# Four-layer decoder on one core: the first attention layer without zero-padded rows, row maxima in two parts, value bias behind the softmax

## The reference

```python
x = x + tanh(g_xattn[l]) * attention_l(layernorm(x), ctx)
x = x + tanh(g_ffn[l])   * feed_forward_l(layernorm(x))
```

```python
q = Wq @ xn + bq;  k = Wk @ ctx + bk;  v = Wv @ ctx + bv      # (128, 256)
p = softmax(q.T k / sqrt(8)) per head;  out = Wo @ (p v) + bo
```

## Time and profile before

| | us |
|---|---|
| median of 3 runs | 1309.64 (1308.12 to 1316.08) |
| profiled execution | 1303.64 |
| its span (first to last instruction) | 1301.7 |
| mean granted TensorE clock | 0.859 of full |
| busy in the span: PE / PEld | 971.2 / 569.7 |
| busy in the span: DVE / ACT / POOL | 685.3 / 439.5 / 376.7 |

### The profile page before, as it was taken

The page is one execution under the profiler, slowest core; times in us unless marked ns, Lnnn a source line. Parts: engine busy times, 40 slices in busy tenths (PEclk is TensorE's granted clock), DMA queues, the critical chain, the costliest instruction groups (busy, mean ns, idle before and its releaser), DMA issues.

```text
span 1301.7 us, 19061 instructions
## 1 busy us (share of the span) xinstructions
PE 971.2 (75%) x6613; PEld 569.7 (44%) x6613; DVE 685.3 (53%) x1700; ACT 439.5 (34%) x718; POOL 376.7 (29%) x516
## 2 busy tenths in 40 slices
PE   1768896788168799577747771598989999559993
PEld 1334453677124345455425651134444544326662
DVE  4858774443378614267662233787878783301111
ACT  4245554211025520244311330035555657212220
POOL 3112210222555100334204004325555656220002
PEclk9989988799669999788657995569989999679997
DMA  5444633364544100644332764201010000530002
GB/s 133 111 94 103 166 103 115 130 227 150 151 113 122 30 24 0 170 74 86 61 129 97 195 180 143 68 6 38 2 38 1 2 2 2 226 126 25 17 13 73
DMA packets 117257, 115.43 MB, mean 89 GB/s; under 512 B 71758, under 2 KB 107342, under 8 KB 113742
## 3 DMA queue, kind: packets, MB, share of 16 engines
q1 hardware_dynamic: 110924, 102.94, 28.8%
q0 software_dynamic: 3072, 8.39, 2.1%
q10 hardware_dynamic: 3168, 2.88, 0.7%
HBM read 88.22 MB, written 29.62 MB: 91 GB/s over the span
## 4 chain that ended last, share of the span: by engine, by line
PE 44%; DVE 18%; issue 9%; DMA 5%; POOL 3%; ACT 2%; SPq 1%; POOLq 0%; DVEq 0%; ACTq 0%
PE psT L1373 6%; PE psT L1083 5%; PE psB L1083 5%; PE psT L1226 4%; PE psB L1192 4%; DVE mxp L1739 4%; PE psO L1270 3%; PE psB L1387 3%; DVE mxp L1743 3%; DMA xn<-scr_sorted 2%; PE psB L1414 2%; PE psB L1438 2%; PE psO L1260 2%; PE psT L1336 1%; PE psB L1091 1%
## 5 line engine op out<-in xcount | busy, mean ns | idle before, releaser
L1519 ACT ACTIVATE Pt<-psT 128x1024 f32<-128x1024 f32 x192 | 195.9, 1023 | 138.8 <-PE psT L1226 136.9
L1739 DVE TENSOR_REDUCE mxp<-psB 128x1 f32<-128x512 f32 x256 | 162.4, 685 | 41.6 <-PE psB L1192 40.4
L1226 PE MATMUL psT<-whole 99*128 99x256 bf16 (+1 forms) x1024 | 156.5, 279 | 10.3 <-issue 10.0
L1743 DVE TENSOR_REDUCE mxp<-psB 128x2 f32<-128x512 f32 x192 | 122.6, 684 | 40.5 <-PE psB L1198 40.1
L1198 PE MATMUL psB<-whole 96*128 96x256 bf16 x384 | 76.9, 308 | 66.3 <-issue 53.3
L1226 PEld LDWEIGHTS psT<-whole 99*128 99x128 bf16 (+1 forms) x1024 | 97.8, 103 | 60.2 <-issue 28.1
L2057 POOL TENSOR_TENSOR rstd<-vare,cst 128x1 f32<-128x1 f32 x64 | 35.9, 563 | 288.9 <-DVE vare L1658 288.6
L1192 PE MATMUL psB<-whole 96*128 96x512 bf16 x256 | 97.5, 438 | 4.8 <-DVE mxp L1739 3.5
L1091 PE MATMUL psB<-cst,xn 128*128 128x128 f32 x96 | 22.9, 330 | 82.3 <-DVE xn L1598 82.0
L1373 PE MATMUL psT<-whole,qf 128*128 x176 | 80.7, 602 | 0.6 <-ACT qf L1558 0.6
L1198 PEld LDWEIGHTS psB<-whole 96*128 96x128 bf16 x384 | 30.2, 105 | 116.4 <-issue 75.7
(11 more groups left out here) (295 smaller groups left out, 1788.6 us busy)
## 6 DMA issues: line engine op xcount, KB each, us to landing
whole<-in_w SPq DMA_DIRECT2D x6, 3072.0 KB, 10.6
whole<-in_w SPq DMA_DIRECT2D x32, 512.0 KB, 4.8
scr_q<-sq SPq DMA_DIRECT2D x48, 96.0 KB, 1.9
scr_k<-sk SPq DMA_DIRECT2D x48, 96.0 KB, 1.9
whole<-scr_q SPq DMA_DIRECT2D x64, 64.0 KB
whole<-scr_k SPq DMA_DIRECT2D x64, 64.0 KB
xn<-scr_sorted SPq DMA_DIRECT2D x31, 128.0 KB, 3.0
scr_sorted_out<-xn SPq DMA_DIRECT2D x31, 128.0 KB, 2.7
```

The lines of the kernel that those rows point to most:

```text
L1226: ins = pe.matmul(psT[:, s.n % 2, i * A.T:(i + 1) * A.T], lhsT=k_at[:, h * kw + s.c * P:h * kw + (s.c + 1) * P], rhs=q_at[:, h * A.T:(h + ...
L1519: act.activation(p_slot(A, s.p)[:, 0:4 * A.T], psT[:, s.n % 2, 0:4 * A.T], ACT.Exp).then_inc(T_used[s.n % 2], 1)
L1739: dve.tensor_reduce(mxp[:, s.un.g % 2, at:at + 1], psB[:, s.n % BANKS, :], AX.X, ALU.max).then_inc(bank_used[s.n % BANKS], 1)
L1743: dve.tensor_reduce(mxp[:, s.un.g % 2, at:at + 2], psB[:, s.n % BANKS, :].rearrange("p (h n) -> p h n", h=2), AX.X, ALU.max).then_inc(bank ...
```

## The change

Six edits, here in the order of the code:

- `Layer` gets `rows` = 6d and `lows`, the number of parts of the maximum: 3 in layer 3, 2 in layers 0 and 1, none in layer 2. The maxima matmul of layer 0 has 48 rows, the score matmul 50; in layers 1, 2 and 3 they have 96, and 98, 96 and 99.
- The steps `zero` go. GpSimd fills the whole value buffer and its ones columns before its first wait.
- negsplit works from the maxima directly: two VectorE operations for two parts, four for three. negmax has two or three DMAs; ln 255 becomes the bias of layer 3's exponential.
- The value bias leaves the values. Since each row of probabilities sums to one, it is a constant per output channel: Wo @ bv. In `prepare` TensorE transposes the row `bv0`, in the new step `bias_out` it multiplies by Wo, and VectorE adds `bo0` and applies the gate. A new step `bias`, one a unit, adds the column to `x` on GpSimd.
- fv of layer 0 is copied by ScalarE; oy of layer 0 is one VectorE operation on `x`.
- Normalising is one operation over both position tiles.

The diff, with little of what stands around each edit; the new fields of `Layer`, the declarations of the tile `ln255` (128x1) and of semaphores, and the count `neg_after` of the DMAs that a wait on the maxima needs are left out.

```diff
@@ -110,7 +110,8 @@
     return Layer(layer=layer, H=heads, d=d, U=units, nb=batches, TC=tcs, T=tcs * P,
-                           NC=chunks, has_max=has_max, G=heads // 4, halves=heads * d // P, parts=2 if layer == 3 else 1)
+                           NC=chunks, has_max=has_max, G=heads // 4, halves=heads * d // P, parts=2 if layer == 3 else 1,
+                           rows=6 * d, lows=(3 if layer == 3 else 2) if has_max else 0)
@@ -418,10 +419,11 @@
                         (packs, u + at["packs"], u + at["packs"] + 0.02)]
+            if A.layer == 0:
+                streams += [([lambda r=units[u]: add("bias", un=r)], u + at["body"], u + at["body"])]
             if A.layer == 0 and u == 0:
-                streams += [([lambda i=i: add("zero", i=i)], w, w)
-                            for i, w in ((0, 0.5 * at["front"]), (1, at["max"] + 0.2), (2, at["max"] + 0.5))]
-                streams += [([lambda: add("prepare")], at["front"], at["front"]),
+                streams += [([lambda: add("prepare", m=take("M"))], at["front"], at["front"]),
+                            ([lambda: add("bias_out", m=take("M"))], at["max_first"], at["max_first"]),
                             ([lambda i=i: add("loads", i=i) for i in range(LOADS)], 2.0, 9.5)]
@@ -934,7 +943,8 @@
                         for r in range(4 if A.layer == 3 else 3):
-                            sp.dma_start(KP[96:99, 4096 * r:4096 * (r + 1)], t["ones3"]).then_inc(k_ones, 16)
+                            sp.dma_start(KP[A.rows:A.rows + A.lows, 4096 * r:4096 * (r + 1)], t["ones3"][0:A.lows, :]
+                                         ).then_inc(k_ones, 16)
                 elif s.kind == "vstore":
@@ -1020,9 +1030,6 @@
                     sp.wait_ge(q_stored[u.g % 2], 32 * (u.g // 2 + 1))
-                    if A.layer == 0 and u.u < 3:
-                        sp.wait_ge(q_zeroed, u.u + 1)
-                        sp.wait_ge(k_zeroed, 2 * (u.u + 1))
                     pack(sp, A, QP[:, u.g % 3, :], scratch(dq, A, u.g), A.T, q_packed[u.g % 2], is_q=True)
@@ -1034,8 +1041,8 @@
                     turn(sp, bank_used, s.m)
-                    for p3 in range(3):
-                        r = 96 + p3
+                    for p3 in range(A.lows):
+                        r = A.rows + p3
                         HP = A.H // A.parts
@@ -1117,6 +1124,12 @@
                     pe.wait_ge(const_in, 16 * 6)
+                    pe.transpose(m_begin(s.m)[:, 0:P], row("bv0"), ident).then_inc(bank_ready[s.m % BANKS], 1)
+                elif s.kind == "bias_out":
+                    dst = m_begin(s.m)
+                    pe.wait_ge(bias_made, 1)
+                    pe.matmul(dst[:, 0:1], lhsT=w_at0[:, 3, :], rhs=colx[:, 3:4], start=True, stop=True
+                              ).then_inc(bank_ready[s.m % BANKS], 1)
                 elif s.kind == "kp":
@@ -1181,7 +1194,7 @@
                 elif s.kind == "smax":
-                    A, u, K = s.A, s.un, 96
+                    A, u, K = s.A, s.un, s.A.rows
                     if s.first:
@@ -1203,16 +1216,16 @@
                     pe.wait_ge(neg_split, s.i + 1)
-                    w = 3 * A.H // A.parts
+                    w = A.lows * A.H // A.parts
                     for tc in range(A.TC):
                     A, u = s.A, s.un
-                    K = 99 if A.has_max else 96
+                    K = A.rows + A.lows
                     if s.neg is not None:
-                        pe.wait_ge(neg_in[s.neg % 2], 48 * (s.neg // 2 + 1))
+                        pe.wait_ge(neg_in[s.neg % 2], neg_after[s.neg])
                     if s.first:
@@ -1451,12 +1464,6 @@
                     act.activation(tg[:, 0:8], rows[:, 0:8], ACT.Tanh).then_inc(gates_done, 1)
-                elif s.kind == "zero":
-
-                    at = 6144 + 2048 * s.i
-                    for p in (32, 64):
-                        act.activation(arena[p:p + 32, at:at + 2048], const("zero")[p:p + 32, :].to_broadcast([32, 2048]),
-                                       ACT.Copy).then_inc(k_zeroed, 1)
                 elif s.kind == "kt":
@@ -1489,6 +1496,14 @@
                     ins.then_inc(bank_used[s.m % BANKS], 1)
+                elif s.kind == "fv" and s.A.layer == 0:
+                    turn(act, bank_ready, s.m)
+                    if s.un.u == 0:
+                        act.wait_ge(v_set, 1)
+                    if s.done_before >= 0:
+                        act.wait_ge(PV_done, s.done_before + 1)
+                    act.activation(VA[:, s.un.g % 3, 0:32, 0:8], m_slot(s.m).rearrange("p (h d) -> p h d", d=8), ACT.Copy
+                                   ).then_inc(bank_used[s.m % BANKS], 1)
                 elif s.kind == "fqt":
@@ -1500,8 +1515,8 @@
                     if s.i >= 2:
-                        act.wait_ge(neg_in[s.i % 2], 48 * (s.i // 2))
-                    w = 3 * A.H // A.parts
+                        act.wait_ge(neg_in[s.i % 2], neg_after[s.i - 2])
+                    w = A.lows * A.H // A.parts
                     act.activation(nmT[0:w, s.i % 2, 0:A.T], m_slot(s.m).bitcast(BF16)[0:w, 0:A.T],
@@ -1516,7 +1531,9 @@
                         turn(act, T_ready, s.n)
-                        act.activation(p_slot(A, s.p)[:, 0:4 * A.T], psT[:, s.n % 2, 0:4 * A.T], ACT.Exp).then_inc(T_used[s.n % 2], 1)
+                        bias = ln255[:, :] if A.layer == 3 else 0.0
+                        act.activation(p_slot(A, s.p)[:, 0:4 * A.T], psT[:, s.n % 2, 0:4 * A.T], ACT.Exp, bias=bias
+                                       ).then_inc(T_used[s.n % 2], 1)
                 elif s.kind == "oev":
@@ -1656,14 +1673,6 @@
                     dve.tensor_scalar(vare[:, b:b + 1], mv[:, b, 1:2], EPS, None, ALU.add).then_inc(var_ready, 1)
-                elif s.kind == "zero":
-
-                    at = 2048 * s.i
-                    link(dve.memset(arena[32:64, at:at + 2048], 0.0))
-                    dve.memset(arena[64:96, at:at + 2048], 0.0).then_inc(q_zeroed, 1)
-
-                    link(dve.memset(VA[:, s.i, :, :], 0.0))
-                    link(dve.memset(VA[:, s.i, :, SUMCOL:SUMCOL + 1], 1.0))
                 elif s.kind == "vblocks":
@@ -1676,6 +1685,16 @@
                     link(dve.tensor_scalar(tg[:, 10:11], tg[:, 6:7], 0.1, None, ALU.mult))
+                    turn(dve, bank_ready, s.m)
+                    dve.tensor_copy(colx[:, 3:4], m_slot(s.m)[:, 0:1]).then_inc(bank_used[s.m % BANKS], 1)
+                    evacuated(dve, s.m)
+                    dve.sem_inc(bias_made, 1)
+                elif s.kind == "bias_out":
+                    turn(dve, bank_ready, s.m)
+                    dve.tensor_scalar(colx[:, 3:4], m_slot(s.m)[:, 0:1], col("bo0"), tg[:, 0:1], ALU.add, ALU.mult
+                                      ).then_inc(bank_used[s.m % BANKS], 1)
+                    evacuated(dve, s.m)
+                    dve.sem_inc(bias_made, 1)
                 elif s.kind == "kp":
@@ -1716,21 +1735,14 @@
                     normalise(s.xn)
-                elif s.kind == "fv":
+                elif s.kind == "fv" and s.A.layer == 2:
                     A, n = s.A, s.m
                         dve.wait_ge(PV_done, s.done_before + 1)
-                    if A.layer == 0:
-                        for c in range(2):
-                            ins = dve.tensor_tensor(VA[:, s.un.g % 3, c * 16:(c + 1) * 16, 0:8],
-                                                    m_slot(n)[:, c * P:(c + 1) * P].rearrange("p (h d) -> p h d", d=8),
-                                                    row("bv0").rearrange("p (h d) -> p h d", d=8), ALU.add)
-                    else:
-                        ins = dve.tensor_tensor(VA[:, s.un.g % 3, 0:16, 0:16],
-                                                m_slot(n).rearrange("p (h d) -> p h d", d=16),
-                                                row("bv2").rearrange("p (h d) -> p h d", d=16), ALU.add)
-                    ins.then_inc(bank_used[n % BANKS], 1)
+                    dve.tensor_tensor(VA[:, s.un.g % 3, 0:16, 0:16], m_slot(n).rearrange("p (h d) -> p h d", d=16),
+                                      row("bv2").rearrange("p (h d) -> p h d", d=16), ALU.add
+                                      ).then_inc(bank_used[n % BANKS], 1)
                 elif s.kind == "smax":
@@ -1754,16 +1766,20 @@
 
-                    link(dve.tensor_scalar(nm[:, 0, 0:w], mx, -1.0, LN255 if A.layer == 3 else 0.0, ALU.mult, ALU.add))
                     if s.m_prev2 is not None:
                         turn(dve, bank_ready, s.m_prev2)
-                    part = npt[:, s.i % 2, 0:3 * w].rearrange("p (t c h) -> p c t h", t=A.TC, c=3)
-                    src = nm[:, 0, 0:w].rearrange("p (t h) -> p t h", t=A.TC)
-                    left = nm[:, 1, 0:w].rearrange("p (t h) -> p t h", t=A.TC)
-                    link(dve.tensor_copy(part[:, 0], src))
-                    link(dve.tensor_tensor(left, src, part[:, 0], ALU.subtract))
```

(55 more changed lines are left out.)

## The result

The changed kernel takes 1363.88 us (median of 4 runs, 1360.04 to 1372.40), the kernel before 1311.22 beside it: the ratio is 1.042, 95% interval 1.037 to 1.047. I had forecast 1298.9, within 1286 to 1311. It is slower by some 53 us. Runs over 1.5% above the fastest of their kernel (here one of rows66 and three of l3_rows66) do not count in the ratios, while medians are of all runs unless it is said otherwise.

The account below looks back on a forecast made before the run. Layer 0 was taken as bound by a loop through TensorE and the packed-row reads, layer 1 by VectorE; −9.2 + 0.6 + 3.5 + 1.3 − 5.4 − 1.5 = −10.7 us gave 1292.9 profiled, 1298.9 as median, range 1286 to 1311.

Parts of the forecast that it names:

- B: Layer 0, 48 and 50 rows: no matmul time gained, tile-shape switches cost 0.6 us at the start and 3.5 in loops.
- The slower rival: Layer 0: 90 added switches at 0.45 us each outweigh the gains, TensorE then bounds the layer; +16.4 us, 1326; chance 0.08.
- break-even price of 0.27 us: Layer 0: cost per added switch at which 90 switches, less 7.5 us of cover, cancel 16.6 us of gains.
- The rule on tiling modes: TensorE: rows and columns choose the mode, and changes drain it; without this rule the sum would be −16.6, not −10.7 us.
- A: Start of layer 0: without zeroing, k comes 3.86 us earlier and VectorE's interruption goes; −9.2 us, GpSimd's fill hidden.
- C: End of layer 0: uncovered switches put 1.8 us on the path, one output operation less saves 0.5; +1.3 us.
- D: Layer 1, maxima in two parts: one DMA issue fewer saves 0.67 us in each of 8 units; −5.4 us, between −3 and −8.
- E: Layer 3: one operation less in each of 8 splittings, exponential's constant free; −1.5 us, between 0 and −4.

Follow-up runs that it names:

- rows66: Changed kernel with 66 and 68 rows in layer 0's maxima and score matmuls and zero fills back, no switch added: 1312.90 us, 1.003 of the kernel before.
- l3_rows66: Kernel before with layer 3's packed blocks reversed and its maxima matmul at 66 rows for 96: 1319.54 us, ratio 1.008.
- rows62: Changed kernel with 62 and 64 rows in layer 0 and zero fills back, added switches present: 1330.70 us, 1.014 of the kernel before.
- rows96_three: Changed kernel with layer 0 back at 96 rows, zero fills back and three-part maxima everywhere: 1309.15 us, 0.999 of the kernel before.
- before_two_parts: Kernel before with only two-part maxima in layers 0 and 1, one operation less in layer 3, ln 255 as exponential's bias: 1301.82 us, ratio 0.996.
- before_one_norm: Kernel before with only the normalising made one operation over both position tiles: 1309.21 us, ratio 1.000.
- rows48_filled: Changed kernel with its 48 and 50 rows in layer 0, but zero fills back: 1370.85 us, 1.048 of the kernel before.

## Why the prediction was wrong

- **B failed**, and in one assumption. "The columns streamed are the same, so I take no gain in matmul time" was worked at the clock of the earlier trace rows, 1.00, as if that were a property of the stage. With 48 rows it became 0.50. The sum's term was +3.5; measured, layer 0 lost 63 us from unit 2 on. From first maxima matmul to first maxima matmul the units, beginning with unit 2, lost 6.4, 5.2, 8.0, 12.6 and 12.7 us (the last two 32.4 for 19.8), and the rest of the layer, from unit 7's first maxima matmul to the last output projection, 18.3. The switches themselves, the part that I had counted so closely, came out near their price (20.6 to 20.8 us a unit in rows62, 20.5 worked out). I had also taken 19.8 us for the period of the whole layer; in the kernel before it goes from 24.0 (unit 1) down to 19.8.
- **The slower rival** had the right place and the right sign, at a chance of 0.08, with a time of 1326. It charged the switches, and their break-even price of 0.27 us was never reached at the upper level (0.09, 0.10 more for f32). The mechanism was the lower level, in which TensorE saturates and everything on it costs up to double. I mentioned a low clock there only as something that the switch might meet. Its sign did come true: no idle time left on TensorE in layer 0 and a period above 22.
- **The rule on tiling modes** that I weighed was true and led me to the smaller part. The Trainium skill, "TensorE: Matmul & The Clock Gate", section What's actually happening, has the gate follow how busy TensorE has been recently. In this case TensorE was busy 32.36 of 32.41 us by the profile and stayed at 0.50, so busy time as the profile shows it does not decide alone. The rows in use do count (62 and 48 rows, above). The same page of the Trainium skill, section Why this matters for your kernels, has a matmul over 32 rows take as long as one over 128, and the upper-level rows here agree for 48 and 96 (0.39 and 0.38 us a pair).
- **A** was right in its mechanism: k copied at 11.07 (forecast 11.3), reductions unbroken, unit 1's first maxima matmul at 42.12 (42 to 43). By unit 2 the gain was 6.9 us for 8.6. TensorE was still at the lower level there, where the kernel before had the upper from 55.0, and had more switches; which of the two took the rest is not shown. The fill on GpSimd took 2.66 us for my 3.1 and was hidden.
- **C**: the tail ran almost wholly at the lower level (0.50 from 215 to 249 us, 0.63 to 275) and lost 18.3 us, so my +1.3 cannot be tested. The value copy, the additions and the single output operation did no harm (rows96_three).
- **D** was mis-sized. Layer 1 gave some 1.7 us in the changed kernel and 3.5 in the profile of before_two_parts, for 5.4. These are single executions, and the same stretch came out 5 us longer in that of rows96_three, which keeps the three parts; the firmer number is 4.8 for 6.9 of D and E together, by the ratio of before_two_parts. The chain of waits in layer 1, of the kernel before and of the changed one, names what came next:

```profile
by line: DVE mxp L1743 45.7%; DVE On L1786 6.5%; issue 5.0%; DVE npt L1766 4.2%; DVE x L1792 4.1%; DVE st L1656 3.6%; ACT Pt L1519 3.4%; PE psB L1091 3.4%; DVE rden L1782 3.1%; PE psB L1208 2.7%; PE psB L1286 2.6%; DVE nm L1764 2.4%; DVE nm
```

```profile
by line: DVE mxp L1755 20.7%; PE psO L1271 17.1%; PE psT L1239 14.6%; ACT Pt L1535 13.8%; issue 13.0%; PE psB L1211 6.5%; PE psB L1290 3.5%; PE psB L1098 2.7%; PE psB L1299 2.1%; ACT Oe L1542 1.3%; DVE x L1807 0.8%; PE psB L1221 0.8%; DVE s
```

VectorE's maxima fall from 45.7% to 20.7% of the chain, and TensorE's value and score products with ScalarE's exponential (17.1, 14.6 and 13.8%) take over. I had only looked at the DMA queue as the next bound.

- **E**: layer 3 came out 2.6 us shorter for 1.5, but that is not shown to be E: in the profile of before_one_norm, which leaves the splitting as it was, the same stretch is 3.0 shorter. One of E's statements was wrong, "The constant in ScalarE's exponential costs nothing": it costs 91 ns each time, as the last fence of this document shows.

## What to carry to other kernels

Before taking rows out of a matmul, ask what the stage's clock rests on: with TensorE busy 82% of a steady stretch, a halved row count cost more than the zeros ever did, though at an equal clock a pair of 48-row matmuls took 0.39 us and a pair of 96-row ones 0.38. Fewer rows saved no time on TensorE here, so the zero fill was better moved to where engines wait for inputs than removed. And when TensorE is near the bound, a forecast needs the price of its lower clock level as a case of its own, worked as the stage's whole TensorE time at that level.

## What the runs showed of the hardware

- The granted clock depends on the rows in use: with instructions, switches and fills the same, 62 rows gave 1330.7 us and 74.9 of 150 us at the lower level, 48 rows 1370.9 and all 150. Between 96 and 66 rows, without any added switch, it was 1302.1 and 30.7, 1312.9 and 53.8. From 98 to 128 rows in the score matmul nothing changed (27.3 in both).
- TensorE can be busy for well over 100 us on end by the profile and stay at the lower level: in rows48_filled from 60 to 239 us with no idle gap above 0.15 us, in the changed kernel from 130 to 249 with one of 1.2 us.
- An exponential of 128x1024 with a constant out of a tile as its bias takes 91 ns more than one without. Of the changed kernel's page, layers 0 and 1 and then layer 3:

```profile
L1535 ACT ACTIVATE Pt<-psT 128x1024 f32<-128x1024 f32 x96 | 97.9, 1023 | 102.7 <-PE psT L1239 102.6
...
L1535 ACT ACTIVATE Pt<-psT,ln 128x1024 f32<-128x1024 f32 x96 | 106.5, 1114 | 55.0 <-PE psT L1239 54.1
```

In the kernel before all 192 take 1023 ns, those of layer 3 too. Most of it is hidden in layer 3, whose chain is TensorE's to 69% in the changed kernel. The exponential's own part of that chain went from 0.8% of 266 us to 2.2% of 264, some 4 us. The Trainium skill, "ScalarE: Activation LUTs", section What ACT_TABLE_LOAD costs, gives about 93 ns for such an operand; the rows agree.
